# Attention on one core: output turned by DMA, a half-precision output product, and steps moved between the four tiles of a group

## What is computed

```python
q = split_heads(x @ Wq + bq); k = split_heads(x @ Wk + bk); v = split_heads(x @ Wv + bv)
scores = jnp.einsum('bhqd,bhkd->bhqk', q, k) / np.float32(np.sqrt(HD))
scores = jnp.where(adj[:, None, :, :] > 0, scores, jnp.float32(NEG))
attn = jax.nn.softmax(scores, axis=-1)
out = jnp.einsum('bhqk,bhkd->bhqd', attn, v)
...
x = x + gnn(layernorm(x), adj, ...)     # out @ Wo + bo
x = x + ffn(layernorm(x), ...)          # shared expert + routed experts
```

## Time and profile before

| | us |
|---|---|
| median of 3 runs | 1313.75 (1313.02 to 1314.17) |
| the profiled execution | 1311.53 |
| its span, first to last instruction | 1309.70 |

### The profile page before, as it was taken

The page is one execution under the profiler, slowest core; times in us unless marked ns, Lnnn a source line. Parts: engine busy times, 40 slices in busy tenths (PEclk is TensorE's granted clock), DMA queues, the critical chain, the costliest instruction groups (busy, mean ns, idle before and its releaser), DMA issues. The chain is left out here.

```text
span 1309.7 us, 39699 instructions
## 1 busy us (share of the span) xinstructions
PE 1091.0 (83%) x12580; PEld 785.5 (60%) x12581; DVE 993.0 (76%) x2407; ACT 865.8 (66%) x1705; POOL 853.1 (65%) x897
## 2 busy tenths in 40 slices
PE   0799999999999999993489999799999999989200
PEld 0466666666666666662267677577777777778100
DVE  3578888888888888884486988577777777667498
ACT  0688888888888888871368788566766666567000
POOL 3235777877777777857667777177777777766300
PEclk9999999999999999996689999899999999989655
DMA  3123333333333333222335553354444444333399
GB/s 78 33 58 82 92 91 97 85 82 94 90 91 96 96 89 88 70 60 67 107 102 162 144 159 99 59 107 101 97 99 93 99 97 97 77 66 82 120 354 306
DMA packets 273476, 136.51 MB, mean 104 GB/s; under 512 B 192070, under 2 KB 251628, under 8 KB 273402
## 3 DMA queue, kind: packets, MB, share of 16 engines
q1 hardware_dynamic: 239866, 93.38, 29.8%
q0 software_dynamic: 16896, 33.86, 8.1%
q10 hardware_dynamic: 16640, 8.39, 2.1%
HBM read 47.95 MB, written 54.04 MB: 78 GB/s over the span
## 5 line engine op out<-in xcount | busy, mean ns | idle before, releaser
L1376 POOL DMA_INDIRECT pairs_dram<-x_rows x272 | 279.3, 1027 | 123.7 <-issue 83.8
L1054 ACT ACTIVATE hid<-Z,biases 128x512 f32<-128x512 f32 (+1 forms) x336 | 208.0, 631 | 139.4 <-PE Z L1022 96.3
L1069 DVE SCALAR_TENSOR_TENSOR h<-hid,h 128x512 f16<-128x512 f32 (+1 forms) x288 | 183.5, 649 | 52.8 <-ACT h L1045 48.1
L473 DVE TENSOR_REDUCE smin<-S 128x8 f32<-128x1024 f32 x128 | 155.7, 1217 | 80.5 <-PE S L739 79.0
L1034 PEld LDWEIGHTS Y<-w,h 128*128 128x128 f16 x3168 | 186.8, 99 | 27.3 <-issue 10.2
L1034 PE MATMUL Y<-w,h 128*128 (+1 forms) x3168 | 193.5, 221 | 11.3 <-DVE h L1069 9.1
L1167 POOL DMA_INDIRECT slots_dram<-x_rows,pair_slot x128 | 131.7, 1029 | 47.5 <-issue 24.7
L1022 PE MATMUL Z<-x_rows,w 128*128 128x512 f16 (+1 forms) x720 | 150.1, 355 | 10.9 <-issue 7.8
L334 POOL DMA_INDIRECT slots_dram<-x_rows,pair_slot x116 | 118.7, 1024 | 28.8 <-issue 16.6
L476 DVE TENSOR_TENSOR probs<-smin,S 128x768 f32<-128x768 f32 x128 | 122.2, 954 | 14.4
L1045 ACT ACTIVATE h<-hid 128x512 f16<-128x512 f32 (+1 forms) x176 | 105.8, 601 | 20.7 <-ACT hid L1054 5.4
(11 more groups left out here) (212 smaller groups left out, 2185.5 us busy)
## 6 DMA issues: line engine op xcount, KB each, us to landing
y_pairs<-pairs_dram SPq DMA_DIRECT2D x32, 512.0 KB, 6.0
x_res<-in_x_dram SPq DMA_DIRECT2D x32, 256.0 KB, 3.3
adj<-in_adj_dram SPq DMA_DIRECT2D x32, 256.0 KB
xT_dram<-xT SPq DMA_DIRECT2D x32, 256.0 KB, 3.4
xTu<-xT_dram SPq DMA_DIRECT2D x32, 256.0 KB
out_dram<-x_res ACTq DMA_DIRECT2D x16, 512.0 KB, 8.3
pairs_dram<-x_rows POOLq DMA_INDIRECT x272
slots_dram<-x_rows,pair_slot POOLq DMA_INDIRECT x256, 2.4
```

The lines of the kernel that those rows point to most:

```text
L473: dve.tensor_reduce(smin[:].rearrange("p (r e) -> p r e", e=2), S_heads, AX_X, ALU.min).then_inc(s["min_done"], 1)
L1054: act.activation(self.hid[:, c, 0:w], self.bank(b, c)[:, 0:w], ACT.Gelu, bias=bias[:, c:c + 1], scale=1.0 / (XS * WS)).then_inc(self.gelu_ ...
L1069: dve.scalar_tensor_tensor(out=self.piece(b)[:, 1, c, 0:w], in0=self.hid[:, c, 0:w], scalar=HS, in1=self.piece(b)[:, 0, c, 0:w], op0=ALU.m ...
L1376: pool.indirect_dma_start(pairs_dram, bass.IndirectOffsetOnAxis(ap=pair_of[n][:, j:j + 1], axis=0), y_sb[n % NY][:, j], None, bounds_check ...
```

## The change

The attention output is turned by a DMA instead of PE. For that it is split into two half-precision tensors, like the other operands of products: ACT makes the high half (`high_output`, into `at16`), DVE the low half (`low_output`, the output less its high half), SP turns both (`turn_output`, `aT16`), and the output product becomes three half-precision products a tile, with `wo16`. V is kept 64 times larger, so that the halves hold it; the residual divides by that (a `scalar_tensor_tensor` in place of a `tensor_tensor`). Only the last group's output is still turned by PE. The direct exponentials were two heads before and are two now.

Steps move in every engine's list. PE: V's product of a tile comes between the two halves of the turned probabilities in tiles 0 to 2, K's product at the end of tile 2, the logits (now of group g-4) at the end of tile 0. ACT: V's evacuation goes to the next group's tile 0, the logits' to tile 1, the normed rows' high half from the end of tile 3 to tile 2. DVE: `stats2` and `gather2` go from tile 3 to tile 2, `mask` from tile 2 to the end of tile 3, `low_output` is new in tile 3. POOL: the norm comes behind the first scatter, the other three behind the norm. SP: the turnings come ahead of the loads.

```diff
     probs = sb("probs", [P, 2, H, P])
     pT = sb("pT", [P, 2, H, P])
     oT = sb("oT", [P, 2, P])
-    attn = sb("attn", [P, 2, GT, H, HD])
-    attnT = sb("attnT", [P, GT * P])
-    wq, wk, wv, bias_rest, bo_rows, bv_mat, out_bias, ones = (
-        attn[:, n // GT, n % GT].rearrange("p h c -> p (h c)") for n in range(2 * GT))
-    before = attnT[:, 0:P]
+    attn = sb("attn", [P, GT, H, HD])
+    at16 = sb("at16", [P, GT, 2, P], F16)
+    aT16 = sb("aT16", [P, GT, 2, P], F16)
+    wo16 = sb("wo16", [P, 2, P], F16)
+    wq, wk, wv, bias_rest = (attn[:, n].rearrange("p h c -> p (h c)") for n in range(GT))
+    bo_rows, bv_mat, out_bias, ones = (at16[:, n].rearrange("p a c -> p (a c)").bitcast(F32) for n in range(GT))
+    before = aT16[:, 0].rearrange("p a c -> p (a c)").bitcast(F32)
     xc2 = xn
     xT = sb("xT", [P, 2, 2, GT * P], F16)
...
@@ -235,6 +239,13 @@
             sp.dma_start_transpose(xnT[:, g % 2].rearrange("p j a t -> p (j a) t"),
                                    xn16[:, :, :, :].rearrange("p j a c -> p (j a c)")).then_inc(s["xnT_in"], 16)
 
+        def turn_output(g):
+
+            wait(sp, "asplit_done", g + 1)
+            wait(sp, "out_ps", g)
+            sp.dma_start_transpose(aT16[:, :, :, :].rearrange("p j a t -> p (j a) t"),
+                                   at16[:, :, :, :].rearrange("p j a c -> p (j a c)")).then_inc(s["aT_in"], 16)
+
         for g in range(3):
             load_x(g)
...
@@ -242,19 +253,23 @@
         turn_normed(0)
         turn_normed(1)
         for g in range(3, 6):
+            turn_normed(g - 1)
+            if g >= 4:
+                turn_output(g - 4)
             load_adj(g)
             load_x(g + 1)
-            turn_normed(g - 1)
         load_x(7)
         turn_rows(0)
         for g in range(6, NG + 5):
+            if g - 1 < NG:
+                turn_normed(g - 1)
+            if g - 4 < NG - 1:
+                turn_output(g - 4)
             if g < NG:
                 load_adj(g)
             if g + 2 < NG:
                 load_x(g + 2)
             store_xT(g - 6)
...
                 scatter(g - 5, 0, g * GT)
-            if late:
-                scatter(g - 5, 1, g * GT + 1)
             if has(g, -2):
                 norm1(g + 2, g % 2)
             if late:
+                scatter(g - 5, 1, g * GT + 1)
                 scatter(g - 5, 2)
+                scatter(g - 5, 3)
             if has(g, -2):
                 low_half(g + 2)
             if has(g, 2):
                 split(g - 2)
-            if late:
-                scatter(g - 5, 3)
         for g in range(NG - 5, SENT):
             for j in range(GT):
                 scatter(g, j)
...
@@ -430,7 +443,14 @@
             wait(dve, "out_ps", g + 1)
             wait(dve, "xc1_done", g + 1)
             xg = x_res[:, bass.ds(g * GT, GT), :]
-            dve.tensor_tensor(xg, bank[:, :].rearrange("p (j c) -> p j c", j=GT), xg, ALU.add).then_inc(s["x2_done"], 1)
+            dve.scalar_tensor_tensor(out=xg, in0=bank[:, :].rearrange("p (j c) -> p j c", j=GT), scalar=1.0 / (XS * WS),
+                                     in1=xg, op0=ALU.mult, op1=ALU.add).then_inc(s["x2_done"], 1)
+
+        def low_output(g):
+
+            wait(dve, "ahi_done", g + 1)
+            dve.tensor_tensor(at16[:, :, 1], attn[:, :, :, :].rearrange("p j h c -> p j (h c)"), at16[:, :, 0],
+                              ALU.subtract).then_inc(s["asplit_done"], 1)
 
         def stats2(g):
...
@@ -527,13 +547,15 @@
                     residual(g - 2)
                 if j == 3 and has(g, 4):
                     place(g - 4, q)
+                if j == 3 and has(g, 1):
+                    low_output(g - 1)
                 if j % 2 == 0 and has(g, 1):
                     normalise((g - 1) * 2 + j // 2, g - 1, 1 - q, j)
-                if j == 2 and has(g, -1):
-                    mask(g + 1, 1 - q)
-                if j == 3 and has(g, 2):
+                if j == 2 and has(g, 2):
                     stats2(g - 2)
                     gather2(g - 2)
+                if j == 3 and has(g, -1):
+                    mask(g + 1, 1 - q)
                 if j == 1 and has(g, 4):
                     choose(g - 4, q)
...
@@ -567,6 +591,13 @@
             wait(act, "xn_ready", g + 1)
             wait(act, "xnT_in", g * 16)
             act.activation(xn16[:, :, 0], xn[:], ACT.Copy).then_inc(s["xhi_done"], 1)
+
+        def high_output(g):
+
+            wait(act, "norm_done", (g + 1) * GT // 2)
+            wait(act, "aT_in", g * 16)
+            act.activation(at16[:, :, 0], attn[:, :, :, :].rearrange("p j h c -> p j (h c)"), ACT.Copy)\
+                .then_inc(s["ahi_done"], 1)
 
         def evac(task, g, q):
...
                         last = act.activation(probs[:, j % 2, h], S_heads[:, h // 2, h % 2], ACT.Exp,
                                               bias=smin[:, h:h + 1], scale=-1.0)
                     last.then_inc(s["direct_done"], 1)
-                if a and has(a[1]):
-                    evac(*a)
+                if j == 2 and has(g, -2) and not (isinstance(g, int) and g < 0):
+                    high_half(g + 2)
+                if j == 3 and has(g, 1):
+                    high_output(g - 1)
                 if has(t, 1, NT):
                     act.activation(pT[:, (j - 1) % 2, HH:H], keep_transposed(t - 1, 1), ACT.Copy).then_inc(s["pt_sb"], 1)
                 if has(t, 0, NT):
@@ -627,18 +656,17 @@
                 if has(t, 2, NT):
                     wait(act, "pv_ps", t - 1)
                     act.activation(oT[:], OD[:, 0:2 * P].rearrange("p (a t) -> p a t", a=2), ACT.Copy).then_inc(s["o_sb"], 1)
-                if j == 3 and has(g, -2) and not (isinstance(g, int) and g < 0):
-                    high_half(g + 2)
 
         def drain():
             evac("lg", NG - 4, 0)
             act.activation(pT[:, 1, 0:HH], keep_transposed(NT - 1, 0), ACT.Copy).then_inc(s["pt_sb"], 1)
-            evac("aT", NG - 2, 0)
             act.activation(pT[:, 1, HH:H], keep_transposed(NT - 1, 1), ACT.Copy).then_inc(s["pt_sb"], 1)
             for t in (NT - 2, NT - 1):
                 wait(act, "pv_ps", t + 1)
                 act.activation(oT[:], OD[:, 0:2 * P].rearrange("p (a t) -> p a t", a=2), ACT.Copy).then_inc(s["o_sb"], 1)
-            evac("aT", NG - 1, 1)
+            act.wait_ge(last_aT_ps, 1)
+            wait(act, "out_ps", NG - 1)
+            act.activation(aT16[:, :, 0], last_aT, ACT.Copy).then_inc(s["ahi_done"], 1)
             for g in range(NG - 3, NG):
                 evac("lg", g, g % 2)
...
             elif task == "out":
-                wait(pe, "aT_sb", g + 1)
                 bank = last_bank(g, task)
                 if bank is M0:
                     m0_free(pe, task, step_g)
+                else:
+                    wait(pe, "sub_done", NT)
+                    wait(pe, "direct_done", NT)
+                if isinstance(g, int) and g == NG - 1:
+                    wait(pe, "asplit_done", NG)
+                else:
+                    wait(pe, "aT_in", (g + 1) * 16)
                 pe.matmul(bank[:, :].rearrange("p (j c) -> p j c", j=GT), sel[:],
                           bias3[:].unsqueeze(1).to_broadcast([P, GT, P]), start=True, stop=False)
                 for j in range(GT):
-                    mm = pe.matmul(bank[:, j * P:(j + 1) * P], attnT[:, j * P:(j + 1) * P], wo[:], start=False, stop=j == GT - 1)
+                    for n, (k, m) in halves():
+                        mm = pe.matmul(bank[:, j * P:(j + 1) * P], aT16[:, j, m], wo16[:, k],
+                                       start=False, stop=j == GT - 1 and n == 2)
                 mm.then_inc(s["out_ps"], 1)
             elif task == "lg":
...
@@ -721,9 +753,8 @@
         def step(g, q):
             for j in range(GT):
                 t = g * GT + j
-                tasks = {0: (None, ("aT", g - 2, q), None), 1: (None, ("out", g - 2, q), None),
-                         2: (("Q", g + 1, 1 - q), ("K", g + 1, 1 - q), None),
-                         3: (None, ("V", g + 1, 1 - q), ("lg", g - 3, 1 - q))}[j]
+                tasks = {0: (None, None, ("lg", g - 4, q)), 1: (None, ("out", g - 2, q), None),
+                         2: (("Q", g + 1, 1 - q), None, ("K", g + 1, 1 - q)), 3: (None, ("V", g + 1, 1 - q), None)}[j]
                 if has(t, 0, NT):
 
...
@@ -758,6 +789,24 @@
                     for a in range(2):
                         mm = pe.transpose(ON_turned[:, 1 - j % 2, a], oT[:, a], ident[:])
                     mm.then_inc(s["on_ps"], 1)
+                def times_values():
+
+                    if has(t, 2, NT):
+                        vq, vj = (q, j - 2) if j >= 2 else (1 - q, j + 2)
+                        if vj == 0:
+                            wait(pe, "v_sb", g + 1)
+                        wait(pe, "pt_sb", 2 * (t - 1))
+                        wait(pe, "o_sb", t - 2)
+                        if j == 3 and has(g, 4):
```

(24 more changed lines are left out.)

50 lines of the change are left out of this document (22 added, 28 removed).

## The result

The changed kernel takes 1397.2 us (median of 4 runs, 1391.2 to 1402.2) against 1314.0 before: ratio 1.063, 95% interval 1.058 to 1.068. It is slower, as forecast, but by 83 us and not by 56: the time lies 15 us beyond the upper end of the range. The span of the profiled run is 1397.3 us.

The account below looks back on a forecast made before the run. The prediction took a nearly closed chain on DVE as the bound; 27 groups at +2.05 us (55.4), plus 3, less 1.8, made 56.6 on 1311.53, so 1368.1, given as 1370 us; range 1364 to 1382.

Parts of the forecast that it names:

- What bounds the group, and the place of the loss: Between groups: DVE's nearly closed chain bounds; after the change PE's first scores wait for the last tile's mask, +2.05 us a group.
- The chain of holds: Last tile: POOL's split multiplication holds the low half, then POOL's cast goes first and holds the mask; scores at 19.35.
- The loss in the choice: Third tile: POOL's norm multiplication holds DVE's choice of experts until 9.05, losing 0.5 us.
- From the scores to the minimum: Start of a group: DVE's minimum comes 1.29 us after PE's scores start, read from the earlier trace.
- over 1382: Rival, whole run: a late transfer that stops PE as well, or a third hold a group; chance 0.04.
- The mask's wait alone, +0.40 a group: Rival, group's end: without contention PE waits only for the mask, +0.40 a group, 11 us, 1325 us; chance 0.14.
- PE's gain of 0.5 to 0.6: PE's last tile: less work makes PE ready at 16.8 instead of 17.42, alone worth 0.5 to 0.6 us a group.
- The turning by DMA at nothing: SP's queue: the turned output lands 3.0 us after issue, needed some 6 us into the next group; no cost.
- V's product between the halves at nothing: Inside a tile: it fills PE's wait for ACT, but PE then waits for DVE anyway; no cost, no gain.

Follow-up runs that it names:

- moves_undone: Changed kernel, substance kept, with mask, second statistics, POOL's scatters and ACT's high half of the normed rows back in their old places: 1330.9 us.
- moves_undone_sp: moves_undone with SP issuing the turning of the output ahead of that of the normed rows: 1301.8 us.
- v_product_last: Changed kernel with V's product behind both halves of the turned probabilities in the first three tiles too, as before the change: 1399.6 us.
- mask_before_low: Changed kernel with DVE making the mask ahead of the low half, still in the last tile: 1342.8 us.

## Why the prediction was right or wrong

**What bounds the group, and the place of the loss: right.** PE waits for the mask, and the minimum behind it waits for PE.

**The chain of holds: right to a quarter of a microsecond.** Counted as in the prediction, with the group's first minimum at 1.29 (315.73 in the trace, so the origin is 314.44): POOL's norm multiplication 8.07 to 9.11 (forecast 8.0 to 9.05); the split's multiplication 16.87 to 17.91 (16.95 to 18.0); low half ready 16.91, done 18.46 (17.12, 18.55); cast done 18.93 (19.15); mask done 19.22 (19.45); scores 19.56 (19.5, and 19.35 taken). That the scores come so near is in part luck: the mask is 0.23 early, and PE starts 0.34 behind it where the forecast had 0.05. The loss in the choice is 0.4 us, forecast 0.5. The runs show the cause too: with the split delayed, low half and mask fall to 0.69 and 0.42.
The Trainium skill, SBUF — State Buffer, section "Who interferes with whom", says that issue order decides who is blocked. The trace agrees: in the changed kernel POOL's multiplication starts 0.04 us ahead of the low half, which takes 1.55 us, and POOL's cast, held in turn by the low half, takes 0.95.

**From the scores to the minimum: the step that failed.** The sum took +2.05 a group, which says that the minimum again comes 1.29 us after the scores start. That distance was read from the earlier trace rows, where PE had waited 0.16 us. But the forecast itself made PE wait: ready at 16.8, scores at 19.35. Behind the real wait (2.19 us) the clock is at 1.2 GHz and the distance is 2.24 us: 0.95 more in each of the groups 6 to 30, 25 x 0.95 = 24 of the 27 us between 1370 and 1397. A group grew by 3.19 us and not by 2.05; the rest of that is the start of the scores, 19.56 instead of 19.35. The kernel with PE kept busy, without the slow clock, takes 1369.7 us. That this is the forecast's 1370 to a microsecond is luck: its groups are 0.1 us shorter than forecast, and its repeats cost about 4 us in the first groups.
The Trainium skill, TensorE: Matmul & The Clock Gate, section "What's actually happening", says that an idle array is put to half its clock. The trace agrees that it happens (0.50 behind the wait of 2.18 to 2.19 us in groups 6 to 29), and not behind every such wait (1.00 behind 2.13 us in group 5); I had not weighed it.

**The bounds and the "over 1382" rival.** Its chance was 0.04, for a late transfer or a third hold. The run is slower than 1382 for neither reason. A slow PE behind the predicted wait belonged among the rivals as a mechanism of its own.

**The mask's wait alone, +0.40 a group: near, as far as shown.** No run is that case, the whole change without holds. The nearest is the kernel with the split later: 18.62, less the 0.85 that the choice is held, is 17.77, an estimate of +0.47 against 17.30. Two other pairs bear on the moves alone: with the substance kept, the mask in the last tile (ahead of the low half) and the statistics in the third cost 0.37 (17.26 against 16.89); in the kernel before, the two DVE moves give +0.12.

**PE's gain of 0.5 to 0.6: near, though not measured alone.** Without the moves and with SP's order mended the substance gives 0.41 a group and 1301.8 us, with the low half on DVE paid.

**The turning by DMA at nothing: right in this kernel, by its order.** Between 100 and 600 us the changed kernel has no wait of PE for it. With the normed rows late and SP's order kept, PE waits 1.04 us for it in the group shown; the order on SP is all that moves_undone and moves_undone_sp differ in, 29 us apart, in which the held masks of moves_undone are included. The prediction named the queue, but not that its place there depends on ACT's high half.

**V's product between the halves at nothing: right in this kernel,** 27 us where PE decides more.

## What to carry to other kernels

When a forecast makes PE wait where it did not wait before, do not price what follows with durations from rows where PE was busy: look at the granted clock behind waits, and where waits of like length show both clocks, as 2.13 and 2.18 us here, carry a case at each. Cheap work on PE during the wait can be worth more than it costs, and waiting later (only for the product that needs the data) more still. When steps move between engines, write down which 128x512 operations of POOL come to lie beside DVE instructions that read two SBUF tensors, or beside one like the mask; moving a single instruction often only moves the meeting.

## What the runs showed of the hardware that was not expected

- In the changed kernel PE's waits of 2.18 and 2.19 us in groups of 20.5 us were followed by a granted clock of 0.50 (334 to 337 us in the group shown), those of 1.70 and 2.13 us in groups 4 and 5 were not. In v_product_last the clock fell behind waits of 1.78 us (scores 1.24 at 193.50) and not behind one of 2.17 (0.71 at 354.76). So the length of the one wait does not settle it; what does was not found. In the three kernels where PE's wait for the mask is 0.9 to 1.24 us, scores and products behind it have their full rate (0.71, 0.61).
- From the mask's end to the scores it is some 0.35 us in the groups of the loop, at either clock (0.34 in the changed kernel, 0.35 in mask_before_low), where PE has two more waits behind the one for the mask, and 0.05 to 0.06 in the two kernels where that wait is the last. What it comes from was not tested.
- A hold goes both ways: POOL's cast takes 0.95 us instead of 0.61 when DVE's low half has gone ahead, and the mask takes 0.83 to 1.42 instead of 0.41, depending on when POOL's operation began.
